# Expert weights split ahead of time, and the activations' low parts moved from VectorE to POOL

## The reference

```python
h = _rmsnorm(x, ln2_w)                     # 1024 tokens x 128
probs = jax.nn.softmax(h @ router_w, axis=-1)
topv, topi = jax.lax.top_k(probs, 2)       # made into weights[token, expert], 0 for six of the eight
gate = jnp.einsum('bsd,edm->bsem', h, w_gate)     # E = 8, M = 448
up = jnp.einsum('bsd,edm->bsem', h, w_up)
act = jax.nn.silu(gate) * up * weights[..., None]
moe = jnp.einsum('bsem,emd->bsd', act, w_down)
return x + moe
```

## Time and profile before

| | us |
|---|---|
| median of three runs | 672.4 (671.8 to 674.63) |
| span of the profiled execution | 672.5 |
| experts, first to last matmul of the units | 526.1 to 664 |

### The profile page before, as it was taken

The page is one execution under the profiler, slowest core; times in us unless marked ns, Lnnn a source line. Parts: engine busy times, 40 slices in busy tenths (PEclk is TensorE's granted clock), DMA queues, the critical chain, the costliest instruction groups (busy, mean ns, idle before and its releaser), DMA issues. The chain is left out here.

```text
span 672.5 us, 11274 instructions
## 1 busy us (share of the span) xinstructions
PE 577.2 (86%) x3380; PEld 449.6 (67%) x3380; DVE 508.6 (76%) x1030; ACT 420.5 (63%) x1024; POOL 326.1 (48%) x606
## 2 busy tenths in 40 slices
PE   2959999999999889998886578999865896979996
PEld 1837778787777767776766456665545684857885
DVE  4657877878788687887796258989844799878994
ACT  2537877778767577786575248888833554544653
POOL 1345767767677656778586364554021506050000
PEclk9979999999999899999898759999985999887998
DMA  7020000001000000000000020000002200200001
GB/s 255 1 57 0 1 33 1 1 2 33 1 1 2 0 1 2 1 1 2 0 2 1 0 91 0 2 1 1 1 2 82 83 1 0 82 0 0 0 0 33
DMA packets 14391, 13.11 MB, mean 19 GB/s; under 512 B 2048, under 2 KB 13696, under 8 KB 14336
## 3 DMA queue, kind: packets, MB, share of 16 engines
q1 hardware_dynamic: 14032, 12.41, 5.8%
q10 hardware_dynamic: 304, 0.03, 0.0%
HBM read 11.92 MB, written 0.52 MB: 19 GB/s over the span
## 5 line engine op out<-in xcount | busy, mean ns | idle before, releaser
L1071 POOL TENSOR_SCALAR attn_probs<-attn_probs,rinv 128x512 f32<-128x512 f32 x128 | 87.4, 695 | 29.4 <-DVE rinv L975 29.4
L848 ACT ACTIVATE attn_probs<-bank,bias 128x512 f32<-128x512 f32 x128 | 87.4, 687 | 10.0 <-DVE bias L968 10.0
L984 DVE TENSOR_TENSOR pT_lo<-bank,pT_hi 128x512 fp32r<-128x512 f32 x128 | 87.3, 683 | 7.3 <-ACT pT_hi L864 5.8
L701 PE MATMUL bank<-ident,attn_probs 128*128 128x128 f32 x512 | 77.6, 285 | 12.4 <-POOL attn_probs L1071 11.8
L960 DVE TENSOR_REDUCE neg_max<-bank 128x1 f32<-128x512 f32 x128 | 81.9, 681 | 6.6 <-PE bank L686 6.6
L864 ACT ACTIVATE pT_hi<-bank 128x512 fp32r<-128x512 f32 x128 | 73.4, 595 | 15.3 <-PE bank L701 15.0
L701 PEld LDWEIGHTS bank<-ident,attn_probs 128*128 128x128 f32 x512 | 57.4, 143 | 36.4 <-POOL attn_probs L1071 21.0
L1904 ACT ACTIVATE act_hi<-act_f 128x512 fp32r<-128x512 f32 x56 | 35.4, 632 | 57.2 <-DVE act_f L1947 56.8
L731 PE MATMUL bank<-pT_hi,vals 128*128 128x256 f32 x256 | 67.7, 296 | 2.2 <-DVE pT_lo L984 1.4
L731 PE MATMUL bank<-pT_lo,vals 128*128 128x256 f32 x256 | 65.6, 288 | 0.0
L731 PEld LDWEIGHTS bank<-pT_hi,vals 128*128 128x128 f32 x256 | 49.9, 195 | 4.3 <-issue 1.7
(11 more groups left out here) (311 smaller groups left out, 1639.3 us busy)
## 6 DMA issues: line engine op xcount, KB each, us to landing
ctx_raw<-in_ctx SPq DMA_DIRECT2D x4, 512.0 KB, 5.0
wkv_raw<-in_L_xattn_Wkv SPq DMA_DIRECT2D x2, 1024.0 KB, 10.4
gu_raw<-in_L_ffn_w_gate SPq DMA_DIRECT2D x4, 448.0 KB, 3.6
gu_raw<-in_L_ffn_w_up SPq DMA_DIRECT2D x4, 448.0 KB, 4.3
dn_raw<-in_L_ffn_w_down SPq DMA_DIRECT2D x4, 448.0 KB, 5.3
x<-in_x SPq DMA_DIRECT2D x1, 512.0 KB, 6.8
wq_raw<-in_L_xattn_Wq SPq DMA_DIRECT2D x1, 512.0 KB, 10.3
wout_raw<-in_L_xattn_Wout SPq DMA_DIRECT2D x1, 512.0 KB, 11.9
```

Source lines behind the costliest of these rows:

```text
L701: last = pe.transpose(t_bank[half][:, j * N + t * P:j * N + (t + 1) * P], probs[:, g % 2, i, t, kt * P:(kt + 1) * P], k.ident[:, :])
L848: act.activation(probs[:, g % 2, i, t, :], score_bank(G, i)[:, :], ACT.Exp, bias=bias[:, t, h:h + 1], scale=X_SCALE, accum_out=row_sum[:, ...
L984: dve.tensor_tensor(pT_lo[:, i, 2 * half:2 * half + 2, :], t_bank[half][:, :].rearrange("p (j n) -> p j n", j=2), f(pT_hi[:, i, 2 * half:2 ...
L1071: pool.tensor_scalar(probs[:, g % 2, i, t, :], probs[:, g % 2, i, t, :], rinv[:, t, h:h + 1], 1.0, ALU.mult, ALU.mult).then_inc(p_norm_s, 1)
```

## The change

`split_pair` writes to a slot for each of the four pairs (`gu_hi`, `gu_lo`, `dn_hi`, `dn_lo` grow from 2 to `PAIRS` slots), and all four pairs are fetched and split inside self-attention. The fetch of pair g waits until pair g-1 is split. POOL's order there becomes: `attention_out(1)`, split 0, out 2, split 1, out 3, `z`, split 2, out 4, split 3, out 5, 6, 7.

In the experts POOL has no splits left; it makes `act_lo` in place of DVE. DVE's order is `weigh(n)`, `product(n)`. The two-turn loop is written out as 56 units, so that counters are constants and nothing drains in the middle. The order on PE and ACT is the same.

```diff
@@ self_attention, sync
-            fetch_pair(sp, k, dram, 0)
+            for g in range(PAIRS):
+                fetch_pair(sp, k, dram, g)
@@ self_attention, gpsimd
             attention_out(1)
-            split_pair(pool, k, 0, 0)
+            split_pair(pool, k, 0)
             attention_out(2)
+            split_pair(pool, k, 1)
             attention_out(3)
             z(range(TT))
-            for h in range(4, SA // HELD):
+            split_pair(pool, k, 2)
+            attention_out(4)
+            split_pair(pool, k, 3)
+            for h in range(5, SA // HELD):
                 attention_out(h)
@@ fetch_pair
+    if g >= 1:
+        sp.wait_ge(k.split_s, g)
@@ experts, gpsimd
-            split_pair(pool, k, 1, 1)
-            with pool.Fori(1, PAIRS // 2) as g:
-                for slot in range(2):
-                    split_pair(pool, k, g * 2 + slot, slot, (down_ps, (g * 2 + slot - 1) * U))
+            for n in range(UNITS):
+                pool.wait_ge(a_hi_s, n + 1)
+                pool.tensor_tensor(act_lo[:, n % 2, :], act_f[:, n % 2, :], f(act_hi[:, n % 2, :]), ALU.subtract).then_inc(a_lo_s, 1)
@@ experts, vector
-            with dve.Fori(0, PAIRS // 2) as g:
...
-                for n in range(2 * U + 1):
-                    if n < 2 * U:
-                        weigh(n)
-                    if n >= 1:
-                        tail(n - 1)
-                    if n < 2 * U:
-                        product(n)
+            for n in range(UNITS):
+                weigh(n)
+                product(n)
@@ build
-        k.gu_hi, k.gu_lo = (sb(f"gu_{s}", [P, 2, 2, 2 * HID], F32R) for s in ("hi", "lo"))
-        k.dn_hi, k.dn_lo = (sb(f"dn_{s}", [P, 2, SLABS, D], F32R) for s in ("hi", "lo"))
+        k.gu_hi, k.gu_lo = (sb(f"gu_{s}", [P, PAIRS, 2, 2 * HID], F32R) for s in ("hi", "lo"))
+        k.dn_hi, k.dn_lo = (sb(f"dn_{s}", [P, PAIRS, SLABS, D], F32R) for s in ("hi", "lo"))
```

More of the change, by code:

```diff
@@ L1750, in fetch_pair, with split_pair @@
 def fetch_pair(sp, k, dram, g):
+    if g >= 1:
+        sp.wait_ge(k.split_s, g)
     for which, name in enumerate(("L0_ffn_w_gate", "L0_ffn_w_up")):
[L1753 to L1759, removed]
-    pool.wait_ge(k.raw_in, (g + 1) * 48)
[L1762 to L1767, removed]
+        sp.dma_start(k.gu_raw[:, which, :, :], dram[name][2 * g:2 * g + 2, :, :].rearrange("e d m -> d e m")).then_inc(k.raw_in, 16)
+    rows = dram["L0_ffn_w_down"][2 * g:2 * g + 2, :, :].rearrange("e m d -> (e m) d")
+    sp.dma_start(k.dn_raw[:, :, :], rows.rearrange("(s r) d -> r s d", r=P)).then_inc(k.raw_in, 16)
+def split_pair(pool, k, g):
+    pool.wait_ge(k.raw_in, (g + 1) * 48)
+    gu_raw = k.gu_raw[:, :, :, :].rearrange("p a e m -> p a (e m)")
+    pool.tensor_tensor(k.dn_hi[:, g, :, :], k.dn_raw[:, :, :], k.one[:, :].unsqueeze(2).broadcast_to([P, SLABS, D]), ALU.mult)
+    pool.tensor_scalar(k.gu_hi[:, g, :, :], gu_raw, 1.0, 1.0, ALU.mult, ALU.mult).then_inc(k.hi_made, 1)
     pool.wait_ge(k.hi_made, g + 1)
[L1769 to L1772, removed]
+    pool.tensor_tensor(k.gu_lo[:, g, :, :], gu_raw, f(k.gu_hi[:, g, :, :]), ALU.subtract)
+    pool.tensor_tensor(k.dn_lo[:, g, :, :], k.dn_raw[:, :, :], f(k.dn_hi[:, g, :, :]), ALU.subtract).then_inc(k.split_s, 1)
 def experts(nc, k, dram, out):
@@ L1803, in experts @@
         PARTS = (slice(0, SPLIT), slice(SPLIT, P))
+        UNITS = PAIRS * U
         def where(n):
@@ L1810, in _ @@
         def _(sp):
-            with sp.Fori(1, PAIRS) as g:
-                sp.wait_ge(k.split_s, g)
-                fetch_pair(sp, k, dram, g)
             for c in range(CH):
@@ L1837, in weight_row, with gate_up, down @@
                 last.then_inc(w_ps, 1)
+            def gate_up(n):
+                g, c, s = where(n)
+                if n >= 3:
+                    pe.wait_ge(silu_s, n - 2)
+                    pe.wait_ge(weighed_s, n - 2)
+                for which, out in ((0, g_bank[n % 3]), (1, u_bank[n % 3])):
+                    for m, (w, x) in enumerate(((k.gu_hi, k.h2T_hi), (k.gu_hi, k.h2T_lo), (k.gu_lo, k.h2T_hi))):
+                        last = pe.matmul(out[:, :], w[:, g, which, s * P:(s + 1) * P],
+                                         x[:, c * BANK:(c + 1) * BANK], start=m == 0, stop=m == 2)
+                last.then_inc(gu_ps, 1)
+            def down(n):
+                g, c, s = where(n)
+                pe.wait_ge(a_lo_s, n + 1)
+                for m, (w, x) in enumerate(((k.dn_hi, act_hi), (k.dn_hi, act_lo), (k.dn_lo, act_hi))):
+                    last = pe.matmul(d_bank[c][:, :], w[:, g, s, :], x[:, n % 2, :], start=False, stop=False)
+                last.then_inc(down_ps, 1)
             pe.wait_ge(wcol_s, 1)
@@ L1843, in _ @@
             pe.wait_ge(w_s2, ROWS // 2)
[L1844 to L1863, removed]
-                    if n < 2 * U:
[L1865 to L1869, removed]
+            for n in range(UNITS + 2):
+                if n < UNITS:
+                    gate_up(n)
+                if n >= 2:
+                    down(n - 2)
             for c in range(CH):
@@ L1880, in _, with mix, silu, head @@
         def _(act):
+            def mix(g, i):
+                act.activation(wide_mix[PARTS[i], g % 2, :], wide[PARTS[i], 2 * g + i, :], ACT.Copy).then_inc(mix_s, 1)
+            def silu(n):
+                act.wait_ge(gu_ps, n + 1)
+                if n >= 2:
+                    act.wait_ge(mul_s, n - 1)
+                act.activation(gate[:, n % 2, :], g_bank[n % 3][:, :], ACT.Silu).then_inc(silu_s, 1)
+            def head(n):
+                act.wait_ge(mul_s, n + 1)
+                if n >= 2:
+                    act.wait_ge(down_ps, n - 1)
+                act.activation(act_hi[:, n % 2, :], act_f[:, n % 2, :], ACT.Copy).then_inc(a_hi_s, 1)
             act.activation(warm[:, :], k.one[:, :], ACT.Silu)
@@ L1887, in _ @@
             act.wait_ge(w_s2, ROWS // 2)
[L1888 to L1904, removed]
-                for n in range(2 * U + 1):
-                    if n >= 1:
-                        head(n - 1)
-                    if n < 2 * U:
-                        silu(n)
-                        if n % U < 2:
-                            mix(n // U, n % U)
+            for n in range(UNITS + 1):
+                if n >= 1:
+                    head(n - 1)
+                if n < UNITS:
+                    silu(n)
+                    if n % U < 2:
+                        mix(n // U, n % U)
             act.wait_ge(sum_ps, 1)
@@ L1919, in _, with weigh, product @@
         def _(dve):
+            def weigh(n):
+                g, c, s = where(n)
+                dve.wait_ge(gu_ps, n + 1)
+                if n >= 2:
+                    dve.wait_ge(mul_s, n - 1)
+                if s == MIXED:
+                    dve.wait_ge(mix_s, g * 2 + 2)
+                    w = wide_mix[:, g % 2, c * BANK:(c + 1) * BANK]
+                else:
+                    w = wide[:, 2 * g + (s > MIXED), c * BANK:(c + 1) * BANK]
+                dve.tensor_tensor(up_w[:, n % 2, :], u_bank[n % 3][:, :], w, ALU.mult).then_inc(weighed_s, 1)
+            def product(n):
+                if n >= 2:
+                    dve.wait_ge(a_lo_s, n - 1)
+                dve.wait_ge(silu_s, n + 1)
+                dve.wait_ge(weighed_s, n + 1)
+                dve.tensor_tensor(act_f[:, n % 2, :], up_w[:, n % 2, :], gate[:, n % 2, :], ALU.mult).then_inc(mul_s, 1)
             dve.tensor_copy(wcol[:, :, :], k.weights[:, :, :].rearrange("p t e -> p e t")).then_inc(wcol_s, 1)
```

## The result

The changed kernel takes 683.15 us (680.83 to 684.21, 4 runs); the kernel before, run beside it, 672.1 us (668.35 to 674.63). The ratio is 1.0178, with a 95% interval from 1.0133 to 1.0222: slower by 1.8%, 11 us. The forecast was 681.4, with 675 to 690 as its range. The profiled executions differ by 9.8 us (spans of 672.5 and 682.3).

What follows compares the result with a forecast made beforehand. PE, at 2.04 us a unit, was taken to bound the expert stage before; after the change, a 2.56 us loop through POOL. Stage +9.1, entry -0.4, self-attention +0.3 gave +9.0 us: 681.4 us, range 675 to 690.

Steps and rivals of the forecast that it cites:

- The bound now, and the hold-up: Expert stage before: PE sets 2.04 us a unit; POOL's splits hold DVE instructions with two SBUF inputs, some 23 us lost.
- The loop: Experts: product, act_hi, POOL's act_lo, next product close a circle of 2.56 us a unit, above PE's 2.04.
- `weigh` beside POOL: Experts, DVE: weigh (0.69 us) fits into POOL's time, as it isn't held.
- POOL is always first: Experts: POOL begins 0.72 us after act_hi starts, gate is there at 1.12, so the product waits for POOL's end.
- PE can't help by running ahead: Experts: the 2.56 us circle holds no step of PE, so PE running ahead doesn't shorten it.
- The sum for the stage: Experts: first product at 529.42, 55 x 2.56 us to the last, stage end at 672.3 against 663.22: +9.1 us.
- Entry: Start of the expert loop: constants for counters cut the 0.51 us before PE's first matmul to 0.07: -0.4 us.
- Self-attention: Three more splits there cost DVE nothing; attention_out(5) comes just too late for DVE's last sums: +0.3 us.
- Span and median: Whole kernel: profiled span (672.5) and median (672.4) taken as the same to 0.1 us, giving 681.4 us.
- Rival A: Experts: POOL doesn't hold the product for so short an instruction, only PE's pace remains: 653 us, chance 0.10.
- Rival B: Experts: the circle closes but is some 0.15 us shorter, so no difference: 673 us, chance 0.05.
- rival C: Experts: PE idles 0.5 us a unit and gets its low clock for half the stage: 709 us, chance 0.04.

Runs made afterwards that it cites:

- the other order: Changed kernel with one more wait on POOL, so act_lo of unit n starts only when the product of unit n+1 is done: 687.88 us, ratio 1.0269.
- the halves: Changed kernel with POOL's act_lo subtraction cut into two instructions of 128x256: 665.22 us, ratio 0.9917.

## Why the prediction was right, step by step

- **The bound now, and the hold-up.** Right. PE at 2.04 us a unit, and with no POOL instruction beside it (low parts on VectorE) the stage runs at that. That only DVE instructions with two SBUF inputs are held was read from seven cases; the gate in PSUM shows it on all 56. That the product ends 0.55 us behind POOL held in all 55 units (0.54 to 0.55).
- **The loop.** 2.56 us were put together from five rows; 2.58 were measured. The terms were 0.03, 0.63, 0.09, 1.26, 0.55; they came to 0.03, 0.63, 0.08, 1.29, 0.55. POOL's was 0.025 us too short and the signal 0.01 too long, 1.1 us over the stage. The Trainium skill's 2.6 cycles an element ("GPSIMD Engine Reference", Performance versus the Vector engine) leave the fixed part of an instruction out and would have given 1.11. As a rate, an estimate of 2.17 ns a column at that page's 1.2 GHz, they agree with the 2.15 of the last section.
- **`weigh` beside POOL.** Wrong, without effect. It does not fit into POOL's time but runs beside `act_hi`, before POOL starts. So `up_w` at 0.69, which was named as a sign, showed nothing in the changed kernel.
- **POOL is always first.** Right in the changed kernel, and for the reason given: with ScalarE's order turned round it never is.
- **PE can't help by running ahead.** Right for this loop (three units of depth: no change).
- **The sum for the stage.** The first `down` of the last unit was put at 663.22 + 9.0 = 672.2; it started at 672.40. That it is so near is partly luck. The first product ended at 528.45 and not at 529.42, a good half of which came from the stages ahead; from there to that `down` 143.95 us passed and not 142.9. The two misses of 1 us cancel.
- **Entry.** -0.4 us was said. From the last `wide` copy to PE's first matmul it was 0.15 us in place of 0.51. That matmul came 0.90 us earlier, at 525.20, and 0.5 of it was there before self-attention began.
- **Self-attention.** +0.3 us was said, 0 came: the transfers took 6.3 us to POOL's start instead of 6.6, and `attention_out(5)` was done some 0.3 us before the sums asked. That margin is narrow.
- **What follows the stage.** It was said not to change. From the last unit's first `down` to the end it took 9.9 us (672.40 to 682.3) where it was 9.3: +0.6.
- **Span and median.** This was the loose step. The span of 672.5 and the median of 672.4 were taken for the same execution's worth, here and in the section on the time before. But a run's time is longer than its span: in the changed kernel the profiled run took 684.21 us with a span of 682.3, 1.9 us more. By that the profiled execution of the kernel before took some 674.4 us and was one of its long ones (longest run 674.63). The spans differ by 9.8 us, near the 9.0 of the sum; the medians differ by 11. The interval of the ratio, 9 to 15 us on 672, holds both.
- **The rivals.** Rival A's time, 653, is close to what the kernel takes once the loop is open: 650.3, 650.5, 652.4 and 653.6 in four different ways. Its price was about right and its condition did not hold. Rival B, a loop shorter by 0.15 us, did not come: 2.58 was measured. The low clock (rival C) did not come while the units ran, up to 670: 1.00 with PE waiting in every unit. It came with the last two `down`: PE waited 1.58 and 1.34 us for them, and from 670.5 to 674 the granted clock was 0.50.

What went wrong lay behind the prediction. That the other order would be free was the main error: the depth of two units, which is no part of the first loop, closes the second one. The same oversight made the forecasts for the halves and for ScalarE's order too low. For the low parts made twice, the product's price to POOL was taken as 0.55 us and is 0.44. For the written-out units, the split that the drain had hidden was left out.

## What to carry to other kernels

Before work is moved from VectorE to GpSimd, look in the trace for VectorE instructions that grow far over their median while GpSimd is busy; the time in which they are held counts as busy, not as waiting. If the instruction that stays behind has two SBUF inputs and follows the moved one in a circle, the two add up instead of overlapping, and a busy share of 48% on GpSimd says nothing of room. Then either keep the work where it was, give the other instruction an operand in PSUM, or arrange the turns and give the chain one more unit of depth: each of the three made the changed kernel 30 us shorter. None of those with `act_lo` on GpSimd came under the 650.3 us of leaving it on VectorE, since TensorE's 2.04 us a unit is the bound in all of them; there was nothing to gain from a shorter VectorE.

## What the runs showed of the hardware

- GpSimd and a VectorE instruction with two SBUF inputs take turns for whole instructions, whoever came first: with GpSimd first the product took 1.34 us in the median, with VectorE first it took 0.69 and GpSimd's subtraction 1.46 in place of 1.29. A held 128x512 instruction of VectorE ended 0.55 us after GpSimd's, and took 0.44 us from it in its turn (1.73 against 1.29).
- A VectorE instruction with one input in PSUM and one in SBUF is not held at all: 0.689 us at most in 56, with GpSimd's 1.29 us around it.
- A hold-up of this kind is not a wait in the profile. It lengthens the record of the held instruction (4.49 us in place of 0.68), and the list of waits does not name the engine that held it.
- GpSimd's subtraction took 0.74 us for 256 columns, 1.26 to 1.29 for 512, 2.1 for 896 and 4.0 for 1792: about 0.16 us and 2.15 ns a column.
